# A four-stage transformer block on one core: another order for the opening, and ternary weights by comparison

## The reference

```python
x = x + quantised_expert(layernorm(x), gu, ctx)      # two int8 linears, silu between
x = x + bitlinear_ffn(layernorm(x), w1, w2, w3)      # ternary weights, width 704
x = x + cross_attention(layernorm(x), ctx, mask)     # 16 heads of 128, 8 kv heads
x = x + moe_ffn(layernorm(x), ...)                   # shared width 1024, routed width 128, top 2 of 8

# quantised linear: s = sqrt(amax_x / amax_w) by column; rows of x/s and w*s are
# scaled to 127, rounded, multiplied, and scaled back
# ternary weights:
gamma = mean(abs(w));  q = clip(round(w / (gamma + 1e-8)), -1, 1)
```

## Time and profile before

| | us |
|---|---|
| median of 3 runs | 456.85 (453.72 to 458.79) |
| the profiled execution, its own time | 456.1 |
| its span, first to last instruction | 454.4 |
| PE busy / DVE busy / ACT busy / POOL busy | 395.8 / 308.2 / 226.6 / 182.2 |

### The profile page before, as it was taken

One profiled execution on the slowest core, in us unless ns is written; L12 is line 12 of the kernel. 1 busy time (PEld: TensorE's weight loads), 2 busy tenths in 40 slices (PEclk: granted clock), 3 DMA queues, 4 the chain that ended last, 5 costly groups with the idle time before them and its releaser, 6 DMA issues.

```text
span 454.4 us, 8501 instructions
## 1 busy us (share of the span) xinstructions
PE 395.8 (87%) x3034; PEld 370.1 (81%) x3034; DVE 308.2 (68%) x929; ACT 226.6 (50%) x622; POOL 182.2 (40%) x300
## 2 busy tenths in 40 slices
PE   0668747699998999999989999999899989998596
PEld 0546636599987998899979997999789979996495
DVE  3479767796786666878765758878665666765343
ACT  0285564456564344656644345656543456564132
POOL 2235283734553433455434334545533332322031
PEclk9988986899999999999999999999999999999699
DMA  7997001000000001100000002000000000000000
GB/s 212 364 343 282 1 0 50 1 2 1 1 0 3 0 1 30 45 1 1 2 1 1 1 1 72 2 1 2 1 1 2 1 23 1 2 2 0 0 1 23
DMA packets 15080, 16.85 MB, mean 37 GB/s; under 512 B 1536, under 2 KB 14016, under 8 KB 15040
## 3 DMA queue, kind: packets, MB, share of 16 engines
q1 hardware_dynamic: 15040, 16.33, 11.1%
HBM read 15.28 MB, written 1.05 MB: 36 GB/s over the span
## 4 chain that ended last, share of the span: by engine, by line
PE 50%; DVE 24%; ACT 12%; POOL 6%; issue 5%; DMA 2%; SPq 1%; DVEq 0%; POOLq 0%; ACTq 0%
PE bank_s L300 13%; PE bank_u L300 10%; PE bank_qa L300 6%; ACT prob L741 6%; DVE prob L1326 5%; PE bank_o L300 4%; PE bank_pt L300 4%; PE bank_pt L471 3%; DVE pt_lo L1337 3%; DVE xn L1140 2%; POOL prob L1000 2%; DVE ut_lo L1343 2%; DMA wq_raw<-in_wqT 2%; ACT ut_hi L707 2%; PE bank_s L568 2%
## 5 line engine op out<-in xcount | busy, mean ns | idle before, releaser
L1000 POOL TENSOR_SCALAR prob<-prob,row_inv,valid_b 128x256 f32<-128x256 f32 x128 | 71.5, 567 | 84.2 <-DVE row_inv L1333 83.6
L741 ACT ACTIVATE prob<-prob,row_min 128x256 f32<-128x256 f32 x128 | 64.1, 502 | 71.5 <-DVE row_min L1326 71.5
L1337 DVE TENSOR_TENSOR pt_lo<-bank_pt,pt_hi 128x512 fp32r<-128x512 f32 x64 | 44.2, 690 | 14.1 <-ACT pt_hi L707 13.8
L1343 DVE TENSOR_TENSOR ut_lo<-bank_u,ut_hi 128x256 fp32r<-128x256 f32 x64 | 27.0, 422 | 38.6 <-ACT ut_hi L707 38.2
L1326 DVE CUSTOM_DVE_ANT_0 prob<-bank_s,masked 128x256 f32<-128x256 f32 x128 | 48.9, 419 | 2.9 <-PE bank_s L300 2.3
L300 PE MATMUL bank_u<-pt_hi,cx_hi 128*128 128x256 f32 x128 | 37.8, 295 | 7.0 <-DVE pt_lo L1337 6.7
L1012 POOL TENSOR_TENSOR act_lo<-act_raw,act_hi 128x256 fp32r<-128x256 f32 x32 | 24.0, 749 | 48.0 <-ACT act_hi L800 48.0
L300 PE MATMUL bank_o<-c_hi,ut_hi 128*128 128x256 f32 x128 | 39.2, 306 | 4.5 <-DVE ut_lo L1343 4.5
L707 ACT ACTIVATE pt_hi<-bank_pt 128x512 fp32r<-128x512 f32 x64 | 37.5, 586 | 10.8 <-PE bank_pt L471 10.8
L471 PE MATMUL bank_pt<-ident,prob 128*128 128x128 f32 x256 | 39.4, 277 | 3.9 <-POOL prob L1000 3.6
L300 PE MATMUL bank_qa<-xt_hi,a_hi 128*128 128x256 f32 x128 | 41.0, 320 | 0.8 <-DVE qa_lo L1315 0.7
(11 more groups left out here) (234 smaller groups left out, 1300.7 us busy)
## 6 DMA issues: line engine op xcount, KB each, us to landing
wq_raw<-in_wqT SPq DMA_DIRECT2D x4, 512.0 KB, 8.8
wo_raw<-in_wo SPq DMA_DIRECT2D x4, 512.0 KB, 9.7
w_raw<-in_w12T SPq DMA_DIRECT2D x1, 1408.0 KB, 9.1
gate_raw<-in_gateT SPq DMA_DIRECT2D x2, 576.0 KB, 8.8
up_raw<-in_upT SPq DMA_DIRECT2D x2, 576.0 KB, 10.5
down_raw<-in_downT SPq DMA_DIRECT2D x2, 576.0 KB, 12.4
x<-in_x SPq DMA_DIRECT2D x4, 256.0 KB, 5.3
guT<-in_guT SPq DMA_DIRECT2D x4, 256.0 KB, 6.8
```

The lines of the kernel that those rows point to most:

```text
L741: last = act.activation(row, row, ACT.Exp, scale=-1.0, bias=row_min[:, h % 2, t:t + 1], accum_out=row_sum[:, h % 2, t:t + 1])
L1000: last = pool.tensor_scalar(row, row, row_inv[:, h % 2, t:t + 1], valid_b[:, 0:1], ALU.mult, ALU.mult)
L1337: dve.tensor_tensor(pt_lo[:, :, :].rearrange("p s t -> p (s t)"), bank["pt"][:, :], f32(pt_hi[:, :, :].rearrange("p s t -> p (s t)")), ALU ...
L1343: dve.tensor_tensor(ut_lo[:, :], bank["u"][:, 0:T], f32(ut_hi[:, :]), ALU.subtract).then_inc(S["u_l"], 1)
```

## The change

1. SP: w12 and w3 are loaded ahead of wkT, wq0, wvT and wo0. guT holds one batch; guT of b+2 is loaded in batch b.
2. Ternary weights by comparison: q = (w > limit) - (w < -limit) with limit = 0.5*(gamma+1e-8). POOL writes (w < -limit), four pieces of 704 columns and w3 in two; DVE makes the rest with one instruction a piece. ACT's passes and the halving of w3 go (the 0.5 is put into `bit_residual`). ACT's magnitudes come first in its program, in six pieces.
3. Batches 1 to 3: `lnq_apply(b)` writes to qw; transposes, maxima, ratio, roots and diagonals of b+2 are made in the feed-forward layer of b (those of batch 1 at the end of the opening); `xn_next`, `q_take` and the twelve transposes go.
4. `q_roots` takes one POOL instruction; batch 0's diagonals are made by DVE (`q_spread_diagonals0`); the silu is two DVE instructions beside ACT's tanh (`q_half_product`, `q_silu`).
5. `prep_unit` uses up to eight banks in turn and its units are spread anew; ACT loads its table with a first small Exp.
6. Feed-forward weights in 12 units of 576 columns, all rests by POOL: unit 0 after `lnb_xn`, 1 to 3 after `lna_xn`, and eight in batch 0's attention, after heads 1, 2, 5, 6, 7, 8, 13, 14.

```diff
-FFN_UNITS = 6
-FFN_LO_POOL, FFN_LO_DVE = (0, 1, 3, 5), (2, 4)
+FFN_LOADS = 6
+FFN_UNITS = 2 * FFN_LOADS
+FFN_LO_HEADS = (1, 2, 5, 6, 7, 8, 13, 14)
@@ PE, opening
             pe.wait_ge(S["consts"], 2)
-            q_turn_x0()
+            q_turn_xn(0)
+            q_piece(0, 0)
             prep_unit(0)
-            q_piece(0, 0)
+            pe.wait_ge(S["abs_done"], 6)
+            pe.matmul(bank["u"][:, 0:6], ones[:, :], gsum[:, :], start=True, stop=True).then_inc(S["gamma_mm"], 1)
+            q_piece(1, 0)
             prep_unit(1)
+            q_piece(2, 0)
...
+            bit_turn(0)
             prep_unit(8)
+            pe.wait_ge(S["w12_ready"], 4)
+            pe.wait_ge(S["prep_lo"], 8)
+            bit_layer(0, beside_bit)          # prep_unit(9) at c == 1, prep_unit(10) at c == 4
...
             queries(0, 1)
+            q_turn_xn(1)
+            prep_unit(14)
             scores(0, 0)
@@ ACT, opening
             for c in range(BIT_CHUNKS):
                 bit_sig(0, c)
                 bit_high(0, c)
-                if c == 0:
-                    prep_hi(12)
-            for u in range(3):
-                ffn_weights_hi(u)
+                if c in (1, 4):
+                    prep_hi(9 + c // 4)
+                elif c in (0, 2):
+                    ffn_weights_hi(4 + c // 2)
@@ POOL, batch
                     if h == 13:
                         power(b + 1, "lnb")
+                    if b == 0 and h in FFN_LO_HEADS:
+                        ffn_weights_lo(FFN_LO_EARLY + FFN_LO_HEADS.index(h))
...
                 for c in range(FFN_CHUNKS - 1):
                     ffn_low(b, c)
+                if b + 2 < NB:
+                    q_roots(b + 2)
+                    q_spread_diagonals(b + 2, 0)
                 if not last:
                     normalise(b + 1, 0)
@@ POOL, opening
+            pool.wait_ge(S["limits"], 1)
+            for j in range(2):
+                for k in range(ND):
+                    ternary12_minus(j, k)
+            q_root1(0)
+            ternary3_minus(0)
+            ternary3_minus(1)
             q_round(0, 1, 0)
...
             power(0, "lnb")
+            pool.wait_ge(S["lnb_xn"], 1)
+            ffn_weights_lo(0)
             for c in range(BIT_CHUNKS):
                 bit_low(0, c)
-            ffn_weights_lo(FFN_LO_POOL[0])
             power(0, "lna")
-            for u in FFN_LO_POOL[1:-1]:
-                ffn_weights_lo(u)
+            pool.wait_ge(S["lna_xn"], 1)
+            ffn_weights_lo(1)
+            ffn_weights_lo(2)
+            ffn_weights_lo(3)
@@ DVE, opening (after the change)
+            ternary_limits()
+            q_bf_w(0)
+            prep_lo(0)
+            prep_lo(1)
+            q_dequant(0, 0).then_inc(S["q_hs"], 1)
+            q_half_product(0)
+            q_silu(0)
+            ternary12(0, 0)
+            q_ratio1(0)
+            ternary12(0, 1)
+            q_spread_diagonals0(1)
+            prep_lo(2)
...
+            ln_apply(0, "lnb")
+            prep_lo(5)
+            ternary12(1, 1)
+            prep_lo(6)
             ln_lo(0, "lnb", xt_hi, xt_lo)
+            prep_lo(7)
+            ternary3(0)
+            ternary3(1)
@@ DVE, the comparison
+            def ternary12(j, k):
+                dve.wait_ge(S["minus12"], 2 * j + k + 1)
+                cols = slice(j * BIT, (j + 1) * BIT)
+                dve.scalar_tensor_tensor(out=w12[:, k, cols], in0=w12_raw[:, k, cols], scalar=above[:, j:j + 1],
+                                         in1=f32(w12[:, k, cols]), op0=ALU.is_gt, op1=ALU.subtract
+                                         ).then_inc(S["w12_ready"], 1)
@@ DVE, feed-forward of batch b
                         if c == 4:
                             mask_row(nxt)
+                            if b + 2 < NB:
+                                lnq_apply(b + 2)
+                        if c == 6 and b + 2 < NB:
+                            q_weight_scales(b + 2)
                         if c == 7:
                             row_minima(nxt, 0)
+                            if b + 2 < NB:
+                                q_first_scales(b + 2)
```

More of the change, by code:

```diff
@@ L696, in _ @@
             queries(0, 3)
+            prep_unit(15)
             for b in range(NB - 1):
@@ L850, in magnitudes, with magnitudes12 @@
                 act.activation(w, raw, ACT.Abs, accum_out=gsum[0:w.shape[0], k:k + 1]).then_inc(S["abs_done"], 1)
+            def magnitudes12(j, k):
+                cols = slice(j * BIT, (j + 1) * BIT)
+                magnitudes(w12[:, k, cols], w12_raw[:, k, cols], 2 * j + k)
             act.wait_ge(S["consts"], 2)
+            act.activation(warm[:, :], ones[:, 0:2], ACT.Exp)
+            act.wait_ge(S["w12_in"], 16)
+            for j in range(2):
+                for k in range(ND):
+                    magnitudes12(j, k)
@@ L861, in _ @@
-            q_tanh(0)
-            magnitudes(w12[:, :, BIT:2 * BIT], w12_raw[:, :, BIT:2 * BIT], 1)
-            act.wait_ge(S["w3_in"], 32)
-            magnitudes(w3[:, 0:BIT_FULL, :], w3_raw[:, 0:BIT_FULL, :], 2)
-            magnitudes(w3[0:BIT_REST, BIT_FULL, :], w3_raw[0:BIT_REST, BIT_FULL, :], 3)
-            prep_hi(4)
-            prep_hi(5)
-            act.wait_ge(S["lnq_shift"], 1)
-            for b in range(1, NB):
-                for t in range(NT):
-                    last = act.activation(xn_next[:, (b - 1) * NT + t, :], x[:, b, t, :], ACT.Identity,
-                                          scale=lnq_rstd[:, b, t:t + 1], bias=lnq_shift[:, b, t:t + 1])
@@ L874, in _ @@
-            last.then_inc(S["next_xn"], 1)
-            prep_hi(6)
-            prep_hi(7)
+            for k in range(4, 7):
+                prep_hi(k)
             q_bf(0, 1)
             q_wscale(0, 1)
+            prep_hi(7)
+            for u in range(3):
+                ffn_weights_hi(u)
+            ln_hi(0, "lnb", xt_hi)
             prep_hi(8)
-            act.wait_ge(S["bit_q12"], 1)
-            for j in range(2):
-                act.activation(w12[:, :, j * BIT:(j + 1) * BIT], w12_raw[:, :, j * BIT:(j + 1) * BIT], ACT.Copy,
-                               bias=-MAGIC).then_inc(S["w12_ready"], 1)
-                if j == 0:
-                    prep_hi(9)
@@ new lines, in ternary3 @@
+            def ternary3(part):
+                dve.wait_ge(S["minus3"], part + 1)
+                rows, cols = ((P, slice(0, BIT_FULL)), (BIT_REST, slice(BIT_FULL, BIT_CHUNKS)))[part]
+                flat = [t[0:rows, cols, :].rearrange("p c d -> p (c d)") for t in (w3, w3_raw)]
+                dve.scalar_tensor_tensor(out=flat[0], in0=flat[1], scalar=above[0:rows, 2:3], in1=f32(flat[0]),
+                                         op0=ALU.is_gt, op1=ALU.subtract).then_inc(S["w3_ready"], 1)
@@ L1608, in _ @@
                 if c == 0:
-                    prep_lo(12)
-                elif 2 <= c < 5:
-                    if c == 2:
-                        dve.wait_ge(S["guT_in"], 16 * (NB - 1))
-                    q_amax0_w(c - 1)
+                    prep_lo(8)
+                elif c == 1:
+                    prep_lo(9)
+                elif c == 2:
+                    lnq_apply(1)
+                elif c == 5:
+                    prep_lo(10)
             bit_residual(0)
             ln_stats_of(0, "lna")
+            prep_lo(11)
+            ln_apply(0, "lna")
+            prep_lo(12)
+            ctx_split_lo(0)
+            ln_lo(0, "lna", xt_hi, xt_lo)
             prep_lo(13)
-            ln_apply(0, "lna")
+            mask_row(0)
+            q_weight_scales(1)
+            queries_lo(0, 0)
             prep_lo(14)
-            ln_lo(0, "lna", xt_hi, xt_lo)
-            ctx_split_lo(0)
-            prep_lo(15)
-            q_ratio0(1, NB)
-            mask_row(0)
-            queries_lo(0, 0)
-            ffn_weights_lo(FFN_LO_DVE[0])
+            row_minima(0, 0)
+            row_minima(0, 1)
+            q_first_scales(1)
+            row_inverses(0, 0)
+            queries_lo(0, 1)
             dve.wait_ge(S["router_hi"], 1)
@@ L1628, in _ @@
                               ).then_inc(S["router_lo"], 1)
-            row_minima(0, 0)
-            row_minima(0, 1)
-            row_inverses(0, 0)
-            queries_lo(0, 1)
-            ffn_weights_lo(FFN_LO_DVE[1])
-            dve.wait_ge(S["q_roots"], 2)
+            prep_lo(15)
             for b in range(NB - 1):
```

452 lines of the change are left out of this document (211 added, 241 removed).

## The result

| | before | after |
|---|---|---|
| median, 20 runs each on one chip | 455.97 (453.72 to 458.79) | 460.16 (458.12 to 463.43) |
| ratio after/before | | 1.0108, 95% interval 1.0087 to 1.0129 |
| span of the profiled execution | 454.4 | 458.7 |
| head 1 of batch 0 turned | 88.4 | 88.2 |
| from there to the end | 366.0 | 370.5 |

The change made the kernel 1.1% slower; I had forecast 448.0, 1.9% faster. The miss is 12.2 us, and it lies in two places: the opening gained 0.2 us where I had 8.8, and what follows lost 4.5 where I had 0.5.

What follows compares the result with a forecast made beforehand. PE bounds the kernel from batch 0's first heads, batch 0's chain the opening. 8.8 us gained by head 1, less 0.5 after, gives 8.3 off 456.1: 447.8, predicted as 448.0, range 443 to 452.5.

Steps and rivals of the forecast that it cites:

- The bound: Whole kernel: PE bounds from batch 0's first heads on; before that, batch 0's chain over all engines bounds the opening.
- the collision: Second linear's diagonals: DVE's tensor_scalar, waiting for POOL's power, loses to POOL's w3 piece, costing 2.1 us; diagonals at 33.5.
- 1.96 us by the equally wide scaling that it replaces: Opening, behind POOL's root: time claimed for `ternary3_minus(0)`, taken from the row of the scaling it replaces.
- The upper end: Second linear's diagonals: cost of DVE losing to POOL, from 0 up to 3.5 us if pieces slowed like down_lo, 3.73 against 2.65.
- The sentence that I left out of the sum: Opening: DVE instructions with two SBUF inputs exclude POOL reading SBUF; `ternary12(1,1)` would wait about 0.6 us, not counted.
- the wait that I credited with 4.8 us: Attention's layernorm: POOL waits for `lna_xn`, so two tensor_scalars take 0.75 us, not 5.31, ending at 64.8 before 69.6.
- The clock: Behind attention's layernorm: PE stays busy enough to run the 12 query products at full clock, 1.4 us instead of 2.7.
- x written: Second linear: x is written by 41.6, before 43.2, a gain of 1.6 us.
- After head 1: Batch 0's head 1 to the end: clock, diagonals, transposes, roots and POOL's rests sum to +0.5 us.
- The first rival (DVE first): Opening: DVE wins the shared moment, or the ternary layer hides ACT's extra work; 2 to 3.5 us back, 445; chance 0.22.
- Late loads: Opening: wq0 lands up to 7.3 us later; half gives 451.7, all 455.3, little or no change; chance 0.16.
- POOL's rests in the heads: Batch 0's attention: eight rests delay normalisations and become the bound, some 10 to 12 us, 459; chance 0.06.

Runs made afterwards that it cites:

- experiment 1: Changed kernel with POOL's six is_lt comparisons replaced by multiply and add of the same shape: 454.45 us, ratio 0.9967 to the kernel before.
- experiment 3: Changed kernel, first ternary comparison on DVE instead of POOL: 454.6 us, ratio 0.9988; or kept on POOL without the multiplication by 1.0: 456.94 us, 1.002.
- experiment 4: Changed kernel with POOL's three feed-forward rests waiting for the low part of attention's layernorm (lna_lo) instead of lna_xn: 458.36 us, ratio 1.0043.
- joined versions: Changed kernel with comparison on DVE, rests behind lna_lo, tiles unshifted, head rests moved; with roots after the next batch's first normalisation 450.44 us, without 450.52.
- experiment 6: Changed kernel with POOL's roots and first diagonals of batch b+2 after batch b+1's first normalisation instead of ahead: 459.86 us, ratio 1.0086.
- Experiment 5: Changed kernel with 56 transposes of a constant tile added on PE ahead of the second linear's spread: 460.33 us, ratio 1.0109.
- experiment 7: Kernel before with tiles shifted 2112 bytes as in the changed kernel: 458.47 us, ratio 1.0053; changed kernel with that shift undone: 458.57 us, 1.0077.
- seven versions: The changed kernel's edited versions from the first six experiments, tiles placed as in the changed kernel: 369.4 to 370.8 us from head 1 to the end.
- experiment 8: Kernel before with only POOL's rests held back, last one moved into attention: until lna_xn 451.89 us, ratio 0.9919; until ctx_lo 453.48 us, 0.9953.

## Why the prediction was wrong, by its own steps

*The bound and the collision: right.* PE was the bound from head 1 on, and the opening was set by batch 0's chain. The collision that I named as the forecast's core (a POOL power, a long POOL instruction behind it, a DVE tensor_scalar waiting for the power) came 0.11 us behind POOL's start, and the 5.31 us of `ln_apply` went as forecast.

*The step that failed: "1.96 us by the equally wide scaling that it replaces".* I priced `ternary3_minus(0)` by the row of another operation of the same width. The four `ternary12_minus` have no term in the prediction at all: its root starts with the ratio, at 30.0, as if POOL were free by then (the expectation of experiment 1 puts what I had reckoned at 1.1 us each). They took 4.60 and 2.64, and the root had to wait until 31.47 for the fourth. The upper end that I gave the cost of that moment, 3.5 us for pieces "slowed as down_lo was", came from slow-down by a neighbour, and no bound was made for the operation's own speed on POOL. Experiments 1 and 3 show that it is the operation on this engine: multiply and add 1.33 and 0.86, DVE 0.88 and 0.57. By the table that is 4.3 us more up to the diagonals than my sum had, 2.3 for the root behind the four pieces and 2.0 for w3's. In the time it is about 6 us by experiments 1 and 3 (1.4% and 1.2%); the 2.1 of the collision, which my sum had, is part of what experiment 3 takes away.

*The sentence that I left out of the sum.* `cx_lo` and `cxT_lo` cost 1.9 us more, and `ternary12(1,1)`, at 1.72 us instead of the 0.94 it takes alone, 0.8 more, both beside a rest on POOL. The Trainium skill's page "SBUF — State Buffer", section "Who interferes with whom", states that a DVE instruction with two SBUF inputs contends with a GpSimd instruction that reads SBUF. For the rests the runs here agree with it: 0.42 against 1.09 and 1.62 us in experiment 4. For POOL's comparisons they agree only in part. The third runs from 26.25 to 28.9 and the fourth from 28.86 to 31.5, and beside them the changed kernel has:

```profile
27.30 0.94 DVE L1576 SCALAR_TENSOR_TENSOR w<-w_raw,above,w 128x704 fp32r<-128x704 f32 x1
...
28.93 1.52 DVE L1576 SCALAR_TENSOR_TENSOR w<-w_raw,above,w 128x704 fp32r<-128x704 f32 x1
```

The first lies wholly inside POOL's instruction and is as long as alone; the second, begun 0.07 us behind POOL's, loses 0.6 us and not the 2.6. I had cited the page, estimated 0.6 us for the one place and left that out since no row of the kernel before showed one. Worse, I applied it to the new comparison alone, and did not ask which DVE instructions come right behind the wait that I credited with 4.8 us. Holding POOL to `lna_xn` moved its 4.5 us of rests onto the next two of them: here part of the stall that went landed on the next in the queue.

*The clock.* I let the 12 query products take 1.4 us; they took 2.90 (2.7 before), at a granted 0.60 from 70 to 80 us. In the joined versions that stretch is granted 1.00. But the late chain is not what made it slow: experiment 6's profile has the changed kernel's opening and grants 0.94 there, with 1.65 us for the products. So 1.3 us of head 1's 8.6 belong to this execution, and why one execution gets the low clock there and another not stays open. From 40 to 50 us the joined versions, without the idling at 30, are granted 0.50, less than the changed kernel's 0.67; a low clock in the opening does not need that gap. Experiment 5 shows that waking PE in one gap does not shorten the chain.

*x written.* From diagonals to x I had 8.1 us, it took 9.5. With the comparison on DVE it is 8.5: about 0.5 is the first spread at the low clock (1.22 against 0.70), 0.4 is POOL's rounding of x beside DVE's (1.48 against 1.11).

*After head 1: +4.5 for +0.5.* 1.6 to 2.4 us are the placement (experiment 7), about 1 is this execution's own (370.5 where the median of the seven versions is 369.5), and 1 to 2 are left for the rest, of which I had 0.5. The placement is what my walk through the diff passed over: a line that only moves a tile from a shared region to a lasting one had no price in it. By place, heads 1 to 15 of batch 0 took 0.7 more (I had 0.5 for the rests) and the boundaries after batches 0 and 1 together 1.2 more, against the 0.9 + 0.4 - 0.8 = 0.5 that I had, part of it placement. From head 1 of the last batch to the end the profiled execution took 84.7 us against 83.1; experiments 4 and 5 took 83.9 and 83.7, so about half of that is placement and the rest this execution's own. That the rests cost little in the heads is argued from head times; no run took them away. The version that was to show it, with each rest made twice, gave no time. Moving the last two out of heads 13 and 14 gave 0.26 us of heads 13 to 15's 0.76.

*Rivals and range.* The first rival (DVE first) did not happen, and not for the pieces' length: with short ones, in experiment 1, the diagonals still came second and took 1.76 us. Late loads did not happen, and POOL's rests in the heads were not the bound. I gave 0.06 to what I did not see, and the three things unseen (an operation's speed, the next instructions in line, addresses) are the result. With the failed prices taken out of the kernel the forecast's mark returns: head 1 is turned at 80.3 and 79.5 in the two joined versions, where I had 79.6. Part of that is luck. These versions do not have the collision of 2.1 us that my 79.6 holds: the second diagonals are there at 31.3 and 29.7, not 33.5, and the lead is gone by DVE's first ternary product, 50.8 and 50.2 against 50.4. I had 8.8 us from x to that product; it took 10.1 in the changed kernel and 11.1 in these, where DVE makes the comparisons too. The time then is 450.4 and not 448.0, for what lies behind head 1.

## What to carry to other kernels

Price an instruction by a row of the same engine and the same operation; equal shape is not enough, and where there is no such row its bounds must be wide. When a wait moves POOL's long work behind a mark, list DVE's next five or so instructions there, the tiny ones too: here tensor_scalars and small subtractions with their inputs in SBUF lasted until POOL's instruction was at its end, while `xt_lo`, with an input in PSUM, kept its 0.68 us. Compare single profiles only after their early marks and the granted clock. And a change that adds or drops tiles shifts others: compare the mean of the bound's main instructions before believing the rest of the story.

## What the runs showed of the hardware

- POOL's tensor_scalar depends on its operations: 128x704 took 0.86 us as multiply and add, 2.2 as `is_lt` alone, 2.64 as `is_lt` and multiply; DVE took 0.57 for the last, and 1.36 beside a rest on POOL.
- A DVE instruction of 12 columns lasted 1.85 us and one of 6 columns 2.30, each beside a POOL subtraction that had begun before it (experiment 8).
- 128x256 products lasted 278 or 282 ns with nothing altered but the address of the moving operand, 2112 bytes further on, 0.5% of the kernel one way and 0.3% the other. Which property of the address does it was not tried.
- Work that keeps PE awake in one gap gave the full clock to the next product (0.70 for 1.22 us), and the one after the next gap was slow instead (1.12 for 0.66).
- The same opening ran its 12 query products at the low clock in one execution, 2.90 us, and at the full clock in another, 1.65 (the changed kernel's profile and experiment 6's).
